# Output projection of a two-layer attention kernel: full matmuls with 128-partition transfers, or 64x64 quarter-array matmuls with transfers of 64 partitions

## The reference

```
def reference(x, ...):
    x = x + _L0_conv_ref(_gn(x), ...)   # attention over 49 pixels, spaced 8 apart
    x = x + _L1_conv_ref(_gn(x), w_out, b_out)
    return x

def _L1_conv_ref(x, w_out, b_out):      # each pixel attends to its 5x5 neighbourhood, 8 heads of 8 channels
    ...
    out = (p * att).sum(axis=3).reshape(N, D, H, W)
    out = jnp.einsum('ndhw,od->nohw', out, w_out) + b_out[None, :, None, None]
    return out
```

## Time and profile before

| | us |
|---|---|
| three runs | 1733.81, 1735.7, 1741.63 |
| median | 1735.7 |
| span of the profiled execution (no other time of it is given) | 1743.6 |
| last stage: from the first load of attention output, issued at 1670.3, to the end | 73.3 |
| TensorE, busy in the whole span | 1434.3 |
| VectorE, busy in the whole span | 1396.1 |
| DMA queue of SyncE | 149.67 MB |

### The profile page before, as it was taken

How to read it: one execution, slowest core, us unless ns; L and a number is a source line. 1 busy time by engine, 2 the same in 40 slices (tenths; PEclk the granted TensorE clock), 3 DMA queues, 4 the chain that set the end, 5 groups by cost and what they waited for, 6 DMA issues and landing times.

```text
span 1743.6 us, 62829 instructions
## 1 busy us (share of the span) xinstructions
PE 1434.3 (82%) x26281; PEld 755.6 (43%) x26281; DVE 1396.1 (80%) x1964; ACT 1030.6 (59%) x1861; POOL 1139.6 (65%) x873
## 2 busy tenths in 40 slices
PE   4989999999999999974597888879797786966754
PEld 2656666666666666651132332323233232322332
DVE  4774777777777777778999999999989999995933
ACT  3554777777777777754564747667474766543300
POOL 5333555555555555530679999999999999985700
PEclk9775999999999999987699999999999999997978
DMA  8702011111104220215202324223232522126079
GB/s 330 301 11 52 18 34 39 28 46 24 50 17 100 21 55 18 55 33 141 52 20 59 98 52 122 52 73 91 58 79 51 122 52 71 39 67 244 22 309 388
DMA packets 106870, 152.35 MB, mean 87 GB/s; under 512 B 71362, under 2 KB 83650, under 8 KB 100034
## 3 DMA queue, kind: packets, MB, share of 16 engines
q1 hardware_dynamic: 106690, 149.67, 29.4%
HBM read 77.99 MB, written 65.20 MB: 82 GB/s over the span
## 4 chain that ended last, share of the span: by engine, by line
PE 44%; DVE 18%; POOL 16%; issue 13%; ACT 5%; SPq 1%; DMA 1%; DVEq 0%; POOLq 0%; ACTq 0%
POOL arena L799 11%; PE PS L1484 7%; PE PS L1321 7%; PE PS L1330 5%; PE PS L1346 5%; DVE arena L1111 4%; PE PS L1298 4%; POOL arena L810 4%; PE PS L1290 4%; DVE arena L1107 4%; PE PS L1507 3%; PE PS L1428 3%; PE PS L1309 2%; PE PS L1360 2%; ACT arena L988 2%
## 5 line engine op out<-in xcount | busy, mean ns | idle before, releaser
L1220 DVE TENSOR_TENSOR arena<-arena,PS 128x1568 f32<-128x1568 f32 x334 | 583.9, 1777 | 16.1 <-PE PS L1484 8.3
L799 POOL TENSOR_TENSOR arena<-arena 128x1568 f32<-128x1568 f32 x168 | 517.7, 3123 | 87.7 <-PE PS L1428 68.1
L765 POOL TENSOR_TENSOR arena<-arena,consts 128x196 f32<-128x196 f32 x512 | 294.3, 609 | 283.7 <-ACT arena L849 283.7
L1484 PE MATMUL PS<-arena,consts 32*32 32x392 f32 x12800 | 396.9, 512 | 78.3 <-DVE arena L1220 23.4
L997 ACT ACTIVATE PS<-arena 128x392 f32<-128x392 f32 x334 | 166.3, 501 | 255.8 <-DVE arena L1220 255.1
L1428 PE MATMUL PS<-arena,consts 128*32 128x392 f32 x1664 | 200.3, 554 | 83.2 <-POOL arena L799 42.1
L1107 DVE TENSOR_REDUCE arena<-PS 128x8 f32<-128x392 f32 x256 | 143.2, 559 | 144.7 <-PE PS L1321 143.2
L1484 PEld LDWEIGHTS PS<-arena,consts 32*32 32x32 f32 x12800 | 145.8, 104 | 246.0 <-issue 96.1
L874 ACT ACTIVATE arena<-PS 128x512 f32<-128x512 f32 x256 | 152.9, 597 | 161.0 <-PE PS L1330 157.2
L810 POOL TENSOR_TENSOR arena<-arena 128x1568 f32<-128x1568 f32 x66 | 202.7, 3081 | 29.4 <-ACT arena L937 20.7
L1330 PE MATMUL PS<-consts,arena 128*128 128x128 f32 x1024 | 177.9, 299 | 0.2
(11 more groups left out here) (109 smaller groups left out, 1724.2 us busy)
## 6 DMA issues: line engine op xcount, KB each, us to landing
arena<-x_wide_dram SPq DMA_DIRECT2D x32, 660.0 KB, 8.2
arena<-x_wide_dram SPq DMA_DIRECT2D x256, 67.5 KB, 2.0
x_wide_dram<-arena SPq DMA_DIRECT2D x12, 1125.0 KB
arena<-in_x_dram SPq DMA_DIRECT2D x8, 1568.0 KB, 14.5
x_wide_dram<-arena SPq DMA_DIRECT2D x64, 196.0 KB, 4.3
x_dram<-arena SPq DMA_DIRECT2D x8, 1568.0 KB, 7.5
attn_dram<-arena SPq DMA_DIRECT2D x256, 49.0 KB, 3.0
arena<-x_dram SPq DMA_DIRECT2D x8, 1568.0 KB, 19.0
```

The lines of the kernel that those rows point to most:

```text
L765: i = nc.gpsimd.tensor_tensor(k_bd[k][:, r], keys.unsqueeze(1).to_broadcast([P, HEADS_T, S]), head_mask.unsqueeze(2).to_broadcast([P, HEAD ...
L799: nc.gpsimd.tensor_tensor(tile, x_part, by, ALU.mult).then_inc(pool_tile, 1)
L1220: nc.vector.tensor_tensor(by_channel(v_tiles[n % V_RING]), shifted_values(half, k), over_channels(PS[:, 2 + n % W_BANKS, 0:PIX]), ALU.mult ...
L1484: mm = nc.tensor.matmul(PS[dst, 4 + i, 0:PIX], ident[src, src], tile[src, c * PIX:(c + 1) * PIX], start=done == 0, stop=done == NK - 1)
```

## The change

In the last stage each image goes through 64 x 64 blocks of the array. Four blocks work on four different quarters: rows by the image (`b2`), columns by the half of the image's pixels (`half`). So the output of one channel has its first 1568 pixels on partition c and the other 1568 on partition 64 + c, and both images of the pair side by side in the free dimension. x1 is loaded in that layout, and the result is stored from it: each of these transfers is replaced by two of 64 partitions, with runs of 6272 B for each image.

```
+    x1_halves = x1_dram.rearrange("(b2 c) bp (g n) -> c bp g b2 n", b2=2, g=2)
+    out_halves = out.rearrange("(bp b2) c h w -> c bp b2 (h w)", b2=2).rearrange("c bp b2 (g n) -> c bp g b2 n", g=2)
...
             def reload_x1(bp):
-                sp.dma_start(x1_in[bp], x1_dram[:, bp, :]).then_inc(x1_reloaded[bp], 16)
+                for g in range(2):
+                    sp.dma_start(x1_in[bp][g * C:(g + 1) * C].rearrange("p (b2 n) -> p b2 n", b2=2),
+                                 x1_halves[:, bp, g]).then_inc(x1_reloaded[bp], 16)
...
             for bp in range(BP):
                 sp.wait_ge(fin_ready, 2 * bp + 2)
-                sp.dma_start(out_rows[:, bp, :], x1_in[bp]).then_inc(out_stored, 16)
-            sp.wait_ge(out_stored, 16 * BP)
+                for g in range(2):
+                    sp.dma_start(out_halves[:, bp, g], x1_in[bp][g * C:(g + 1) * C].rearrange("p (b2 n) -> p b2 n", b2=2)
+                                 ).then_inc(out_stored, 16)
+            sp.wait_ge(out_stored, 32 * BP)
...
             for bp in range(BP):
-                dve.wait_ge(x1_reloaded[bp], 16)
+                dve.wait_ge(x1_reloaded[bp], 32)
                 for g in range(2):
                     dve.wait_ge(fproj, 2 * bp + g + 1)
-                    x1_part = x1_in[bp][:, g * 4 * PIX:(g + 1) * 4 * PIX].rearrange("p (k n) -> p k n", k=4)
-                    nc.vector.scalar_tensor_tensor(out=x1_part, in0=PS[:, 4 * g:4 * g + 4, 0:PIX],
-                                                   scalar=par[:, 4:5], in1=x1_part,
+                    x1_part = x1_in[bp].rearrange("p (b2 q k n) -> p q b2 k n", b2=2, q=2, k=2)[:, g]
+                    summed = PS[:, 4 * g:4 * g + 4].rearrange("p (b2 k) n -> p b2 k n", b2=2)[:, :, :, 0:PIX]
+                    nc.vector.scalar_tensor_tensor(out=x1_part, in0=summed, scalar=par[:, 4:5], in1=x1_part,
...
-                    for k in range(4 * g, 4 * g + 4):
-                        i = nc.tensor.matmul(PS[:, k, 0:PIX], wout_T, at_in[bp][:, k * PIX:(k + 1) * PIX],
-                                             start=True, stop=True)
+                    for k in range(2):
+                        for half in range(2):
+                            for b2 in range(2):
+                                rows, to = slice(b2 * C, (b2 + 1) * C), slice(half * C, (half + 1) * C)
+                                at = (4 * half + 2 * g + k) * PIX
+                                i = nc.tensor.matmul(PS[to, 4 * g + 2 * b2 + k, 0:PIX], wout_T[rows, rows],
+                                                     at_in[bp][rows, at:at + PIX], start=True, stop=True)
                     i.then_inc(fproj, 1)
```

## The result

The changed kernel takes 1767.4 us in the median of 4 runs (1765.3 to 1776.9); the kernel before 1738.1 (1733.8 to 1741.6, 4 runs). The ratio is 1.0178, 95% interval 1.013 to 1.0225: 1.8% slower. Ratios here are computed from the single executions, those in a slower state of the chip left out, and not as the quotient of the medians. The forecast was 1785 with a range of 1752 to 1798, so direction and range held and the size was off: 29 us of the 49 forecast. The forecast's own case was 1775 to 1798, and that did not come; the time lies in the part of the range that was there to take in the rival *Stores keep their rate*.

A forecast was written before the change was run, and what follows sets the result against it. The DMA queue, full at 418 GB/s in the last stage, was taken to bound the kernel, not the engines. Terms of 10.5 and 38.7 us sum to 49.2, added to the median 1735.7: 1785 us, range 1752 to 1798.

The forecast's parts named there:

- The forecast's own case: Reloads and last-stage stores, all on 64 partitions, move at 205 to 220 GB/s; time 1775 to 1798 us; chance 74%.
- Stores keep their rate: Rival: only writing into SBUF suffers, so the last stage pays for 2 loads, 7.7 us; time 1754 us; chance 8%.
- its own signs: Last stage at about 210 GB/s after its loads and some 39 us longer; wrong if its rate is over 300 GB/s.
- the rival of the runs' length: Rival for x1 loads and result stores: run length counts, not partitions; 334 GB/s at 6272 B; time 1746 us; chance 6%.
- the line's fixed part: Length-independent part of a straight line through engine times per run, 201 ns at 2640 B and 472 ns at 12544 B.
- Term 1: Last stage: 2 x1 loads and 8 result stores at 210 GB/s cost 3.87 us more each, +38.7 us.
- Halves overlap: Rival: engines drift so lower and upper halves move together at 425 GB/s; 1736 us, no change; chance 7%.
- Term 2: Attention stage: six early x1 reloads delay the value load behind them 23.2 us; ACT's cover hides 11.9; +10.5 us.

The follow-up runs named there:

- pe_only: Kernel before with only the change's matmuls and VectorE sums, x1 and result transfers as before (output not the reference's); 1733.1 us in one run.
- split_x1: Kernel before with each x1 reload cut in two by partitions, 64 each, runs still 12544 B; 1750.6 us in one run.
- split_columns: Kernel before with each x1 reload cut in two by columns, 128 partitions each, runs of 6272 B; 1752.4 us in one run.
- stores_grouped: Changed kernel with the result stores reordered: the lower halves of all 8 pairs first, then the upper ones; 1772.6 us in one run.
- x1_whole: Changed kernel with x1 kept in DRAM in the last stage's layout: early stores cut in two, reloads on 128 partitions; median 1741.8 us, ratio 1.003 to the kernel before.
- before_later: Kernel before with its early x1 reloads issued behind the spreading of the last head's reciprocals; median 1729.6 us against 1735.6, ratio 0.998.
- stagger: Changed kernel with an extra 0.4 MB DRAM-to-DRAM copy of x1 rows issued ahead of the early reloads; 1750.9 us in one run.
- stores_from_idle: Changed kernel with no result store issued before all 16 sums are made, halves still taking turns; 1781.8 us in one run.

## Why the prediction was right or wrong

**The range held, in part by luck.** The trace places 22.1 us of cost where 49.2 were forecast, 27 us less. The time misses 1785 by only 17.6, since the medians differ by 7 us more than the trace places, and the kernel before came out 2.4 us above the median that the forecast started from. By its own signs the prediction is wrong for the last stage: it named a rate over 300 GB/s as such a sign, and the stores ran at 419; the stage was to grow by some 39 us and grew by 11.2.

**The DMA queue sets the end, TensorE doesn't: right.** pe_only shows it alone, 73.2 against 73.3 us. TensorE's busy time was set too low (25 forecast, 31.7), which costs nothing here.

**Transfers on 64 partitions run at half the rate whatever their runs: right.** 210 was taken, 215 came; split_x1 and split_columns rule out the rival of the runs' length. (One of the two arguments against it in the prediction doesn't hold: the line's fixed part is 129 ns, and the 131 ns of the 2160-byte loads are not under it.) The Trainium skill's port rule ("SBUF — State Buffer", "Door 1: The DMA port swizzle", asymptote 218 GB/s) agrees with the loads here.

**Term 1, the last stage: +38.7 forecast, +11.2 measured. This is the step that failed.** Its part for the two late x1 loads, 7.7 us, was right (split_x1: 8.7). Its part for the eight stores, 30.9 us, was not: "with transfers as long as here I take 210". The mechanism under it holds, since stores_grouped ran at 202 to 216 GB/s. What I had taken over from the loads was that putting the other half right behind doesn't help. For stores it does: they reach 412 to 419 GB/s, and they lost 1.2 us (x1_whole) to 2.5 (the changed kernel against split_x1) in place of 30.9; from an idle queue they took some 16 us to get there and lost 8. The same page of the Trainium skill, section "Can I just issue two DMAs to hit both halves?", says no, with 6% gained. The loads agree with it, the stores do not. My rival *Halves overlap* had named this, but against it stood only rows of loads. *Stores keep their rate* forecast 1754 for the wrong reason: stores_grouped shows that they don't, unless the halves take turns.

**Term 2, ahead of the last stage: +10.5 forecast, +10.9 measured (117.8 - 106.9; 8.6 to 10.9 with the scatter), by another road, so that the match is luck.** L934 was released 21.2 us late, counted from T (23.2 forecast); had it alone held up ACT, L1003 would by these rows have started 9.3 us late, an estimate. But the wait that ended last was VectorE's reciprocal, 10.2 us late, behind TensorE: L934 was through at 1619.32 us and L1003, which needs VectorE's first tile after the reciprocal, started at 1620.24. The prediction took the reciprocal to stay in place: it put at nothing what the longer-filled queue does to TensorE. TensorE was late from three long gaps in which the profile names no releaser. They follow the 16 KB packets of the instruction queue (q8 on the page of the profile, which doesn't name their engine); from the packet records:

| kernel | instruction packet: start, us | ended | TensorE goes on |
|---|---|---|---|
| changed | 1584.60, 1.32 | 1585.92 | 1587.31 |
| changed | 1593.75, 1.39 | 1595.14 | 1596.60 |
| changed | 1602.94, 1.36 | 1604.30 | 1605.83 |
| before | 1586.16, 1.37 | 1587.53 | 1588.39 |
| before | 1594.65, 1.35 | 1596.00 | 1597.35 |

All 34 gaps that the table sums, in twelve kernels, end 0.9 to 1.7 us after such a packet. And from the end of one gap to the end of the next the trace has 255 or 256 TensorE records in 21 of the 22 cases (128 matmuls and as many weight loads, now and then one missing) and 511 in the other, in split_columns: 16384 bytes for 256 records, 64 bytes each. So the gaps come where one packet's worth of instructions is used up. They vanish ahead of the reciprocal when the reloads are issued behind it (0.9 us left in before_later), turn up again beside the moved reloads, and grow with half-rate reloads alone (split_x1). That reloads in the queue cause them is shown; that it is the fetch of instructions behind the data is the one reading at hand that fits all of these rows.

TensorE comes to its batch of 17 matmul records 10.3 us late, counted from T. Of these, 1.2 are lost ahead of the first L1490/L1484 block, 5.4 are gaps, and 3.6 are matmuls that took longer: between that block and that batch they are busy for 16.8 us against 13.2. There the granted clock matters. It stood at 1.00 (2.4 GHz) from 1582.9 to 1596.5 in the kernel before, and the batch of 128 from 1588.39 took 3.68 us; in the changed kernel it fell to 0.50 (1.2 GHz) at 1587.7 and at 1597.9, each time just after TensorE had gone on from a gap, and the batch of 128 from 1596.60 took 5.18 us. Not settled is how much the late value load would cost alone: no run has it late with TensorE on time.

**Sum.** 10.9 + 11.2 = 22.1 us, against 49.2 forecast; the 27 us between them are the stores, to within the scatter.

## What to carry to other kernels

A transfer on half the partitions ran at half the rate in every load here, so count partitions before counting runs, and when a layout change forces halves, put them into stores that take turns or into a stage where the queue is free: x1_whole undid the loss (1.003, 0.998 to 1.008) by moving the halves from the reloads to the early stores. A large prefetch is not free merely because its data aren't needed yet: ask what else comes by DMA at that time, small late loads and, by all that the rows above show, TensorE's instructions, and issue it where TensorE, with its long stream of them, is not about to decide a wait. And a price read from loads says nothing about stores in the same queue; take the two apart before adding them up.

## What was not expected of the hardware

- Stores on 64 partitions whose halves take turns, begun on an idle queue, ran at 246 GB/s at first and at 412 after some 16 us; in the changed kernel the loads stayed at 210 to 218 GB/s (windows of 4 us) while the reloads lasted, some 46 us, and in stagger at 215 after eight copies of 2.1 to 3.0 us had been put ahead of them.
- Ahead of the reciprocal TensorE stood still with no releaser for 5.7 to 6.8 us where the reloads took 23 us, for 8.6 to 11.9 us where they took 46, and for 0 to 0.9 us where none were in the queue. Each gap ended 0.9 to 1.7 us after a 16 KB instruction packet, and 256 TensorE records after the gap before it. The cost at the reciprocal was larger than the gaps: 8.7 us for gaps of 5.9 us.
- Packets of 6272 B took 239 ns in the median in loads on 128 partitions and in stores at full rate, and 488 and 485 ns in the reloads on 64 partitions and in the first 4 us of stores_from_idle.
- Kernels with the same code up to 5 us ahead of T reached it between 1544.6 and 1569.7 us: 25 us apart, where the table puts the change at 22.
